# Query stored as high and low parts, key norm on GpSimd, and buffers at 128-byte multiples in a two-layer macaron transformer

## The reference

```python
x = x + 0.5 * _L0_ffn_ref(_layernorm(x), w12, b12, w3, b3)            # f0a
x = x + _L0_attn_ref(_layernorm(x), Wq, bq, Wk, bk, Wv, bv, Wo, bo, gq, gk)
x = x + 0.5 * _L0_ffn_ref(_layernorm(x), w12, b12, w3, b3)            # f0b
x = x + 0.5 * _L1_ffn_ref(_layernorm(x), w_gate, w_up, w_down)        # f1a
x = x + _L1_attn_ref(_layernorm(x), Wq, bq, ..., Wo, M, z)            # rt
x = x + 0.5 * _L1_ffn_ref(_layernorm(x), w_gate, w_up, w_down)        # f1b

# _L0_attn_ref: 32 heads of 128, S = 1024
q = rms_norm(hidden_states @ Wq + bq, gq)     # over all 4096 columns
k = rms_norm(hidden_states @ Wk + bk, gk)
v = hidden_states @ Wv + bv
attn = softmax(einsum('bhqd,bhkd->bhqk', q, k) / sqrt(128))
out = einsum('bhqk,bhkd->bhqd', attn, v)      # heads side by side
return out @ Wo + bo
```

## The kernel before

| stage | moving | stationary | before | change |
|---|---|---|---|---|
| projections, Q and K | ln_xT | qkv_w parts | 64 and 96 | 0 and 0 |
| projections, V | qkv_w parts | ln_xT | 96 and 64 | 0 and 0 |
| attention, scores | ln_xT_hi (key) | ln_xT_lo (query) | 64 and 64 | 0 and 0 |
| attention, with v | at_pT | at_v | 96 and 96 | 0 and 0 |
| attention, with Wo | at_o | at_y | 96 and 96 | 0 and 0 |
| attention, transposes | ident | at_probs | 0 and 96 | 0 and 0 |
| f0a, f0b, first products | ln_xT | first, f0_w12 parts | 64 and 64 | 0 and 0 |
| f0a, f0b, output product | f0_w3 parts | f0_h parts | 64 and 96 | 0 and 0 |
| f1a, f1b, all | ln_xT, f1_wd parts | f1_w parts, f1_inter | 64 and 64 | 0 and 0 |
| rt, output product | rt_wo parts | rt_ret parts | 96 and 32 | 0 and 0 |

## Time and profile before

### The profile page before, as it was taken

How to read it: one execution, slowest core, us unless ns; L and a number is a source line. 1 busy time by engine, 2 the same in 40 slices (tenths; PEclk the granted TensorE clock), 3 DMA queues, 4 the chain that set the end, 5 groups by cost and what they waited for, 6 DMA issues and landing times. The chain is left out here.

```text
span 2358.3 us, 34122 instructions
## 1 busy us (share of the span) xinstructions
PE 2279.7 (97%) x11044; PEld 1867.9 (79%) x11044; DVE 1639.2 (70%) x2677; ACT 1095.7 (46%) x1782; POOL 754.8 (32%) x705
## 2 busy tenths in 40 slices
PE   7799999999979999999999999999998999899998
PEld 5678888888768888888888888888886788687887
DVE  5533333333379999999999999999986565784665
ACT  3222222222156666666666666666663343352442
POOL 5533322222321111112112111111113466572465
PEclk9999999999999999999999999999999999899999
DMA  2234434344221111111111111111101121131210
GB/s 98 100 136 147 142 136 147 130 146 147 103 85 64 44 50 62 53 40 62 53 40 62 59 34 62 62 40 54 63 23 41 40 77 43 33 124 39 72 58 37
DMA packets 91493, 177.42 MB, mean 75 GB/s; under 512 B 8096, under 2 KB 40864, under 8 KB 87968
## 3 DMA queue, kind: packets, MB, share of 16 engines
q1 hardware_dynamic: 91424, 176.54, 21.8%
HBM read 124.08 MB, written 52.43 MB: 75 GB/s over the span
## 5 line engine op out<-in xcount | busy, mean ns | idle before, releaser
L1004 ACT ACTIVATE at_pT_hi<-ps 128x512 fp32r<-128x512 f32 x512 | 278.3, 597 | 253.0 <-PE ps L1136 252.8
L348 PE MATMUL ps<-ln_xT_hi,ln_xT_lo 128*128 128x512 f32 x1488 | 382.0, 392 | 0.0
L1011 ACT ACTIVATE at_probs<-ps,at_nbias,rms 128x1024 f32<-128x1024 f32 x256 | 309.3, 1208 | 147.9 <-DVE at_nbias L1068 145.1
L348 PEld LDWEIGHTS ps<-ln_xT_hi,ln_xT_lo 128*128 128x128 f32 x1488 | 279.5, 188 | 62.8
L1076 DVE TENSOR_TENSOR at_pT_lo<-ps,at_pT_hi 128x512 fp32r<-128x512 f32 x512 | 326.9, 680 | 1.6 <-ACT at_pT_hi L1004 1.6
L1066 DVE TENSOR_REDUCE at_maxes<-ps 128x1 f32<-128x1024 f32 x256 | 311.4, 1216 | 17.6 <-PE ps L348 15.7
L773 POOL TENSOR_TENSOR qkv_acc<-qkv_acc,qkv_sq 128x512 f32<-128x512 f32 x128 | 165.3, 1292 | 342.7 <-ACT qkv_sq L682 341.4
L1136 PE MATMUL ps<-ident,at_probs 128*128 128x128 f32 x2048 | 265.3, 272 | 3.7 <-DVE at_pT_lo L1076 3.7
L1136 PEld LDWEIGHTS ps<-ident,at_probs 128*128 128x128 f32 x2048 | 238.1, 140 | 38.5 <-issue 5.3
L682 ACT ACTIVATE qkv_sq<-qkv_res 128x512 f32<-128x512 f32 x128 | 80.9, 632 | 372.1 <-DVE qkv_res L737 369.4
L348 PE MATMUL ps<-ln_xT_hi,qkv_w_hi 128*128 128x512 f32 x496 | 197.4, 398 | 12.7 <-DVE qkv_res L737 12.7
(11 more groups left out here) (250 smaller groups left out, 4655.1 us busy)
## 6 DMA issues: line engine op xcount, KB each, us to landing
scratch_q<-qkv_res SPq DMA_DIRECT2D x64, 256.0 KB, 2.0
scratch_k<-qkv_res SPq DMA_DIRECT2D x64, 256.0 KB, 2.0
scratch_v<-qkv_res SPq DMA_DIRECT2D x64, 256.0 KB, 2.3
k_raw<-scratch_k SPq DMA_DIRECT2D x32, 512.0 KB, 4.1
q_raw<-scratch_q SPq DMA_DIRECT2D x32, 512.0 KB, 5.1
at_v_raw<-scratch_v SPq DMA_DIRECT2D x32, 512.0 KB, 3.2
qkv_w<-in_Wq SPq DMA_DIRECT2D x8, 1024.0 KB, 4.9
qkv_w<-in_Wk SPq DMA_DIRECT2D x8, 1024.0 KB, 4.9
```

Of the source, the lines that this page charges most:

```text
L348: last = nc.tensor.matmul(out, s, m, start=(start and n == 0), stop=(stop and n == len(terms) - 1))
L1004: nc.scalar.activation(pT2[jp][0][:, 4 * b:4 * b + 4, w * P:(w + 1) * P], T_BANKS[:, b * HALF:(b + 1) * HALF].rearrange("p (k n) -> p k n" ...
L1011: nc.scalar.activation(probs[l % 4][:], scores(l)[:], ACT.Exp, bias=nbias[:, l % 4:l % 4 + 1], scale=rq[:, l % NT:l % NT + 1], accum_out=s ...
```

## The change

1. *Query.* In the projections ScalarE makes the query's high part times a weight, and VectorE the low part one unit later; SP stores both (two DMAs a unit) to `scratch_q_hi` and `scratch_q_lo` in place of one to `scratch_q`. The weight is gq * gk, the product of both RMS weights, since a score sums query column times key column. Attention loads both parts straight into the operands; VectorE's q_high and q_low go, and TensorE waits for the loads only.
2. *Key.* kn = k_raw * rms without a weight, made by GpSimd at the start of a head's first step.
3. *bv.* 512 columns a group, loaded at the group's start and waited for in its V phase, in place of all 4096 at the beginning.
4. *Starts.* All small buffers are padded to 32 floats or put together in one, so that each buffer starts at a multiple of 128 bytes.

```diff
+LINE = 32
+def whole(n):
+    return (n + LINE - 1) // LINE * LINE
...
-        self.var, self.sd, self.r0, self.corr, self.rstd = (sb(n, [P, NT]) for n in ("var", "sd", "r0", "corr", "rstd"))
+        self.small = sb("small", [P, whole(5 * NT + 1)])
+        self.var, self.sd, self.r0, self.corr, self.rstd = (self.small[:, i * NT:(i + 1) * NT] for i in range(5))
...
-        bv = sb("bv", [P, INNER])
+        bv = sb("bv", [P, HALF])
+        q_hi = [sb(f"q_hi{i}", [P, HALF], F32R) for i in range(4)]
+        q_lo = [sb(f"q_lo{i}", [P, HALF], F32R) for i in range(4)]
...
@@ projections, SP @@
                     if t == Q:
                         load(g, V)
+                        sp.dma_start(bv[:], ins["bv"][bass.ds(g * HALF, HALF)].partition_broadcast(P)).then_inc(bv_in, 16)
...
+                        if t == Q:
+                            sp.wait_ge(q_lo_done, g * UNITS + u + 1)
+                            sp.dma_start(halves("q_hi"), q_hi[u % 4][:].bitcast(F32)).then_inc(q_stored[u % 4], 16)
+                            sp.dma_start(halves("q_lo"), q_lo[u % 4][:].bitcast(F32)).then_inc(q_stored[u % 4], 16)
+                            continue
...
@@ projections, ScalarE, ahead of the square @@
+                        if t == Q:
+                            if u == 0:
+                                act.wait_ge(gain_done, g + 2)
+                            wait(act, q_stored[u % 4], (g * 2 + u // 4) * 32)
+                            nc.scalar.activation(q_hi[u % 4][:], res[u % 4][:], ACT.Copy,
+                                                 scale=gain_now[:, u // 2:u // 2 + 1]).then_inc(q_hi_done, 1)
...
@@ projections, VectorE @@
             v.wait_ge(core.cols_in, 16 * len(core.cols))
-            v.wait_ge(bv_in, 16)
+            nc.vector.tensor_tensor(gain[:], gain[:], core.cols["gk"][:], ALU.mult).then_inc(gain_done, 1)
+            def q_low(g, u):
+                v.wait_ge(q_hi_done, g * UNITS + u + 1)
+                nc.vector.scalar_tensor_tensor(out=q_lo[u % 4][:], in0=res[u % 4][:],
+                                               scalar=gain[:, bass.ds(g * GROUP + u // 2, 1)], in1=q_hi[u % 4][:],
+                                               op0=ALU.mult, op1=ALU.subtract).then_inc(q_lo_done, 1)
...
+                            if t == Q and u >= 1:
+                                q_low(g, u - 1)
+                            elif t == K and u == 0:
+                                q_low(g, UNITS - 1)
...
@@ attention @@
-        k2, q2 = ([(xT[:, 2 * i, :], xT[:, 2 * i + 1, :]) for i in range(2)] for xT in (core.ln.hi, core.ln.lo))
-        v2 = pair("v", [P, NT, HD])
+        k2 = [(core.ln.hi[:, 2 * i, :], core.ln.hi[:, 2 * i + 1, :]) for i in range(2)]
+        q2 = [tuple(part[:] for part in core.q0), (core.ln.lo[:, 0, :], core.ln.lo[:, 1, :])]
+        v2 = [tuple(core.ln.lo[:, k, :].rearrange("p (t d) -> p t d", d=HD) for k in (2, 3)),
+              tuple(sb(n, [P, NT, HD], F32R)[:] for n in ("v_hi", "v_lo"))]
...
-                    wait(sp, q_lo, h)
-                    load(q_raw[:], scratch["q"], h, q_in)
+                    wait(sp, s_scores, (h - 1) * NT)
+                    for part, n in zip(q2[hp], ("q_hi", "q_lo")):
+                        load(part.bitcast(F32), scratch[n], h, q_in[hp])
...
@@ attention, GpSimd, at a head's first step @@
+            def k_norm(h):
+                pool.wait_ge(k_in, h * 16)
+                wait(pool, k_hi, h - 1)
+                nc.gpsimd.tensor_tensor(kn[:], k_raw[:], rk, ALU.mult).then_inc(kn_done, 1)
...
@@ attention, VectorE: k_part, q_high and q_low are gone @@
...
@@ attention, TensorE @@
                     if qt == 0:
-                        pe.wait_ge(q_hi, 2 * i + hp + 1)
-                        pe.wait_ge(q_lo, 2 * i + hp + 1)
+                        wait(pe, q_in[hp], 32 * (i + hp))
```

More of the change, by code:

```diff
@@ L585, in qkv_block @@
         ones = sb("ones", [P, P])
+        gain_now = sb("gain_now", [P, LINE])[:, 0:GROUP]
         bo = sb("bo", [P, DM])
-        bv = sb("bv", [P, INNER])
-        ms, sd, r0, corr, rs = (sb(n, [P, 2, NT]) for n in ("ms", "sd", "r0", "corr", "rs"))
+        bv = sb("bv", [P, HALF])
+        ms, sd, r0, corr, rs = (sb(n, [P, whole(2 * NT)])[:, 0:2 * NT].rearrange("p (a t) -> p a t", a=2)
+                                for n in ("ms", "sd", "r0", "corr", "rs"))
         diag = sb("diag", [P, NT, P])
@@ L602, in qkv_block @@
         weights = [ins["Wq"], ins["Wk"], ins["Wv"]]
-        bias = [core.cols["bq"], core.cols["bk"]]
+        bias, gain = [core.cols["bq"], core.cols["bk"]], core.cols["gq"]
         def groups(eng, body):
@@ L639, in body @@
                         for i in range(4):
-                            sp.wait_ge(stored[i], 6 * 16)
+                            sp.wait_ge(stored[i], 4 * 16)
+                            sp.wait_ge(q_stored[i], 2 * 32)
                         sp.dma_start(core.k_raw[:], scratch["k"][0]).then_inc(k_in, 16)
-                        sp.dma_start(core.q_raw[:], scratch["q"][0]).then_inc(q_in, 16)
+                        for part, n in zip(core.q0, ("q_hi", "q_lo")):
+                            sp.dma_start(part[:].bitcast(F32), scratch[n][0]).then_inc(q_in, 16)
@@ L858, in attention_block @@
         probs = [sb(f"probs{i}", [P, TOK]) for i in range(4)]
-        maxes, nbias, sums = (sb(n, [P, 4]) for n in ("maxes", "nbias", "sums"))
-        rsums = sb("rsums", [P, BODY])
-        k_in, q_in, v_in, o_in = (sem(f"{n}_in") for n in ("k", "q", "v", "o"))
+        small = sb("small", [P, whole(3 * 4 + BODY)])
+        maxes, nbias, sums = (small[:, 4 * i:4 * i + 4] for i in range(3))
+        rsums = small[:, 12:12 + BODY]
+        k_in, v_in, o_in = (sem(f"{n}_in") for n in ("k", "v", "o"))
+        q_in = [sem(f"q{i}_in") for i in range(2)]
         kn_done = sem("kn_done")
-        k_hi, k_lo, q_hi, q_lo, v_hi, v_lo, o_hi, o_lo = (
-            sem(f"{n}_done") for n in ("k_hi", "k_lo", "q_hi", "q_lo", "v_hi", "v_lo", "o_hi", "o_lo"))
+        k_hi, k_lo, v_hi, v_lo, o_hi, o_lo = (
+            sem(f"{n}_done") for n in ("k_hi", "k_lo", "v_hi", "v_lo", "o_hi", "o_lo"))
         s_scores, s_max, s_bias, s_exp, s_rsum = (
@@ L936, in head @@
                 load(o_raw[:], ins["Wo"], h, o_in)
-            head(0)
-            head(1)
-            with sp.Fori(2, HEADS) as h:
-                head(h)
+            head(0, 0)
+            head(1, 1)
+            with sp.Fori(1, HEADS // 2) as i:
+                for hp in range(2):
+                    head(2 * i + hp, hp)
             prefetch.load(sp)
@@ L953, in v_part @@
             def v_part(h, hp):
-                part_lo(v2[hp][1][:], v_raw[:], v2[hp][0][:], v_lo, h + 1, v_hi)
+                part_lo(v2[hp][1], v_raw[:], v2[hp][0], v_lo, h + 1, v_hi)
             def step(i, l):
                 h, hp, there = next_head(i, l)
+                if l % NT == 0 and there:
+                    k_norm(h)
                 if l % NT == 1 and there:
@@ L1095, in step @@
                         ln.vector(v, final(i, l))
-                h, hp, there = next_head(i, l)
-                if l % NT == 0 and there:
-                    k_part(h)
-                if l % NT == 3 and there:
-                    q_high(h, hp)
-                if l % NT == 4 and there:
-                    q_low(h, hp)
             steps(v, step)
@@ L1451, in retrieval_block @@
         raws = [core.first.raw, core.second_raw]
-        w = [core.first] + [Chunk(nc, ctx, f"rt_w{i}", HEADW, raw=raws[i % 2]) for i in range(1, RING)]
-        bq = sb("bq", [P, KVH])
+        w = [core.first] + [Chunk(nc, ctx, f"rt_w{i}", whole(HEADW), raw=raws[i % 2]) for i in range(1, RING)]
+        bq = sb("bq", [P, LINE])
+        den, rden = (bq[:, a:a + 2 * TH].rearrange("p (m t) -> p m t", m=2) for a in (KVH, KVH + 2 * TH))
         WO_RING = 3
```

106 lines of the change are left out of this document (49 added, 57 removed).

## The result

The changed kernel takes **2352.3 us**, median of six runs (2350.1 to 2355.0), the kernel before 2362.8 (2362.0 to 2364.6): ratio 0.9953, 95% interval 0.9942 to 0.9963. It is 10.5 us faster. I had said 2326, in a range of 2308 to 2351: right in sign, too large by 26 us, and the result lies just outside the range, next to rival A.

| stage | before | change | difference |
|---|---|---|---|
| to TensorE's restart in the projections | 118.76 | 115.77 | -3.0 |
| projections, to their last matmul's end | 535.5 | 538.3 | +2.8 |
| stop ahead of attention | 5.85 | 3.69 | -2.2 |
| attention, to the first Wo product after its last stop | 1127.3 | 1121.8 | -5.5 |
| the rest, to the end of the span | 571.0 | 570.3 | -0.6 |

The account below looks back on a forecast made before the run. TensorE, by matmul start-to-start distance, was taken to bound projections and attention. Terms -14.9 - 6.3 - 2 - 7.5 - 3 - 2.2 - 2 = -38 us gave 2322 from the profiled 2360.2, stated as 2326 against the median; range 2308 to 2351.

Parts of the forecast that it names:

- rival A: Whole kernel: buffer starts do nothing, only the non-start terms remain, 2349 us; chance 10%.
- Starts, projections: Projections: starts at 128 bytes make all operand pairings equal, 6.6 ns less on 2256 matmuls, -14.9 us.
- Starts, attention: Attention: 25 ns less in each of 250 steps, -6.3 us; bounds 0 and, if settling after transposes went too, -15.
- Starts elsewhere: Output products of f0a and f0b and the retrieval stage: gain part of 6.6 ns each, -2 us.
- VectorE in attention: Attention: three passes leave VectorE's queue and TensorE's stall of 0.26 us a head goes, 29 heads, -7.5 us.
- First head: Attention's first head, before TensorE is the bound: 3.3 us of VectorE's work goes, counted as -2 us.
- Key norm on GpSimd: Attention: one more GpSimd pass of 2.40 us a head, covered, 0 us.
- Rival C: Attention: GpSimd's key norm makes VectorE stand still 2.4 us a head, +74, so 2400 us; chance 4%.
- Query in two parts: Projections and attention: extra passes, stores and loads are covered, 0 us; uncovered low parts, 0.46 us each, would cost +29.
- Entry: Start of the projections: VectorE no longer waits for the 2 MB load of bv, -3.0 us.
- into attention: Stop ahead of attention: query parts lie ready, so TensorE no longer waits for q_high and q_low, -2.2 us.

Follow-up runs that it names:

- a256: Changed kernel with 128 bytes more behind the RMS factors, putting the projections' weights 256 bytes off the tokens modulo 512: 2324.6 us.
- a512: Changed kernel with two small buffers lengthened so that the products' operands start at one phase modulo 512 bytes: 2323.5 us.
- b128: Kernel before with only item 4 of the change, buffers starting at multiples of 128 bytes: 2363.1 us.
- a32: Changed kernel with its buffers rounded to 32 bytes in place of 128: 2353.5 us.
- run 12: Changed kernel with the key norm of heads 1 to 31 moved back to VectorE: 2355.3 us.
- run 11: Changed kernel with operands at one phase modulo 512 bytes, and the key norm of heads 1 to 31 back on VectorE: 2333.1 us.
- b640: Kernel before with buffers at multiples of 128 bytes and all products' operands at one phase modulo 512 bytes: 2346.9 us.
- b512: Kernel before with only two small buffers lengthened, so that operands start at one phase (64) modulo 512 bytes: 2348.8 us.

## Why the prediction was wrong

*Starts, projections, -14.9.* **This step failed.** "All pairings become equal" is false: they become equal modulo 128 and stay 128 apart modulo 256, and a256 against a512 and the changed kernel shows that 256 is the modulus. The gain was real and sized well (a512: -14.6), but this change doesn't reach it. The rows read then, phases 64 with 64 and 64 with 96, couldn't tell 128 from 256 or 512, since no pair was off by 128; I took the modulus from the wording of the change. Measured for the stage: +2.8, none of it from the starts. It is the clock, granted lower for a while: in the changed kernel the granted clock is 0.64 from 629 to 632 us and 0.50 from 632.37 to 636.37, beside and after the 32 one-column sums of squares. The sums take 4.7 us where they took 3.5, and the ten matmuls after them, most of them 0.427 us apart, take 1.9 us more than before. The profile of before has 1.00 there:

```profile
631.00:634.40 3.40, 3.40 (x33) 3.40 (x31) 0.69 (x1) 0.00 (x0) 0.00 (x0) 1.00 0.56 175
634.40:638.40 4.00, 4.00 (x19) 3.26 (x19) 0.77 (x2) 0.06 (x1) 0.00 (x0) 1.00 0.00 0
```

The kernel b128, which takes the time of before, has the low clock there too, and so have the profiles of all the other kernels here; before's alone hasn't. So I don't count it to the change.

*Starts, attention, -6.3.* Wrong in sign: +18 ns a step in place of -25, 256 steps, +4.6. The same error of modulus: attention's pairs of 512 columns were in phase already, and the new places of the query and the values (item 1 of the change) put the even heads' 128 off. Rounding to 32 bytes in place of 128 leaves it so (a32). In phase, and with the identity 128 off, a step is 34 ns shorter than a plain one of before (a512), -8.7, and 52 ns shorter than the changed kernel's, -13.3: the settling that I had as the bound of -15 is real, but this change doesn't reach it.

*Starts elsewhere, -2.* Only the retrieval's output product came into phase (from 224 with 32 to 128 with 128, modulo 256); f0's stays 128 off, at 232 ns. Thirty intervals of the retrieval's, before and with the change:

```profile
2153.58 0.40 PE L348 MATMUL ps<-rt_wo_lo,rt_ret_hi 128*128 128x512 f32 x1
...
2160.58 0.40 PE L348 MATMUL ps<-rt_wo_lo,rt_ret_hi 128*128 128x512 f32 x1
```

```profile
2145.74 0.39 PE L356 MATMUL ps<-rt_wo_lo,rt_ret_hi 128*128 128x512 f32 x1
...
2152.55 0.39 PE L356 MATMUL ps<-rt_wo_lo,rt_ret_hi 128*128 128x512 f32 x1
```

7.00 / 30 = 0.2333 us became 6.81 / 30 = 0.2270. So inside the changed kernel, too, the pace rose where the two starts came into phase modulo 256, and only there; and 64 bytes off (224 with 32) had cost what 32 and 128 do. It is worth some 1.5 us; measured for all of the rest, with stretches at the lower clock that lie elsewhere: -0.6.

*VectorE in attention, -7.5.* Right: stall gone, TensorE 1000.00 of 1000 us, 0.26 us a head. A head took 34.88 us and takes 34.77: -0.26 from the stall, +0.15 from the phase. *First head, -2.* Right: from its first scores to those of the second 34.18 us against 36.21.

*Key norm on GpSimd, 0.* Right. VectorE's reduction takes 1222 ns in the mean between 900 and 1500 us against 1216, its other passes the same to a nanosecond, while GpSimd has one pass of 128x1024 more. Rival C had nothing. What the move is worth depends on the stream: 3.0 us here, 4.5 by the traces (run 12), 9.6 in phase (run 11).

*Query in two parts, 0.* Right; TensorE has no idle row there. Of the +29 that I kept as a possible price, the low part shows 773 - 743 = 30 ns over its median in the mean, not 460. That isn't because the two engines share well. Where a low part meets an addition of GpSimd, it waits:

```profile
246.93 1.29 POOL L821 TENSOR_TENSOR qkv_acc<-qkv_acc,qkv_sq 128x512 f32<-128x512 f32 x1 [24.78 <-ACT qkv_sq L710]
...
247.77 1.00 DVE L757 SCALAR_TENSOR_TENSOR qkv_q_lo<-qkv_res,col_gq,qkv_q_hi 128x512 fp32r<-128x512 f32 x1
```

It ends 0.55 us after the addition, and so do all the long ones, up to 1467 ns; but of the 64 only some 15 meet an addition, hence the median of 743. The Trainium skill's rule that two such instructions block each other (SBUF — State Buffer, Who interferes with whom) agrees with this. I could have seen it before: the additions that ran beside w_lo at the entry in the earlier trace rows (of bo, not of squares) take 1264 ns in the median and 3317 at the longest.

*Entry, -3.0, and into attention, -2.2.* Right: -3.4 in the stop (9.21, I said 9.7; 0.4 came back ahead of it), and 3.69 where I said 3.6.

*The sum.* -3.0 - 2.2 - 5.5 - 0.6 + 2.8 = -8.5. (The medians are 10.5 apart; the profiled execution of before took 2.6 us less than its median and has no low clock after the sums.) Without the three terms on starts my sum was -14.7, which is rival A's 2349; with attention's +4.6 it is -10.1. A was right that starts give nothing in the projections here, but not in its reason, for starts do much, and that the time came out so near to A's number is in part luck. It had 10% and deserved more: the forecast rested on a correlation with two values. The range failed by 1.3 us at its upper end, which was A's own number with no room for attention becoming slower. The Trainium skill's lines of 16 bytes (SBUF — State Buffer, Specifications) don't give a period of 256; the measurements decide.

*The parts add up badly.* Everything but the starts gave 10.5 us at the slow pace (b128 to the changed kernel 10.8), and 23.4 in phase (b640 to a512). The phase gives 15.5 us without the change (b512) and 28.8 with it (a512), 13.3 more. Of these, 4.6 only undo what the change itself had put out of phase in attention. The other 8.7 are the faster settling: b640's plain steps have it too (4.29 us), but there VectorE's three passes hold TensorE up for 0.44 us a head, and with the change they are gone. Each part takes away the limit that hides the other.
